# Moving context work and a layer's first groups into the preceding feed-forward in a four-layer transformer kernel

## The reference, cut to what matters

```python
# layer 0 (layer 1 has the same form), heads of 16 numbers
h1 = _modulate(_ln(x), sh_msa, sc_msa);  x = x + (_attend(qkv of h1) @ W_proj + b_proj)
h2 = _modulate(_ln(x), sh_x, sc_x);      x = x + (_attend(h2 @ W_q, ctx @ W_k, ctx @ W_v) @ W_out + b_out)
h3 = _modulate(_ln(x), sh_mlp, sc_mlp);  x = x + (gelu(h3 @ W_fc1 + b_fc1) @ W_fc2 + b_fc2)
# layer 2, heads of 64 numbers, with rotary positions
ctx_n = _ln(context, ca_lnc_w, ca_lnc_b)
k, v = jnp.split(ctx_n @ wkv, 2, axis=-1);  k = _rope(_heads(k), sk, ck)
# layer 3, heads of 64 numbers, no rotary positions
k = (ctx @ Wk).reshape(b, j, heads, -1);  v = (ctx @ Wv).reshape(b, j, heads, -1)
```

## Time and profile before

| | us |
|---|---|
| median of 3 runs | 5055.48 |
| range of the runs | 5040.6 to 5058.69 |
| the profiled execution, its time | 5061.33 |
| the profiled execution, its span from first to last instruction | 5059.5 |
| PE busy | 4276.2 (85%) |
| DVE busy | 3428.3 (68%) |
| ACT busy | 1869.3 (37%) |
| POOL busy | 1266.7 (25%) |
| mean granted TensorE clock | 0.913 |

### The profile page before, as it was taken

The page is one execution under the profiler, slowest core; times in us unless marked ns, Lnnn a source line. Parts: engine busy times, 40 slices in busy tenths (PEclk is TensorE's granted clock), DMA queues, the critical chain, the costliest instruction groups (busy, mean ns, idle before and its releaser), DMA issues.

```text
span 5059.5 us, 55363 instructions
## 1 busy us (share of the span) xinstructions
PE 4276.2 (85%) x20572; PEld 2524.0 (50%) x20572; DVE 3428.3 (68%) x4976; ACT 1869.3 (37%) x2692; POOL 1266.7 (25%) x600
## 2 busy tenths in 40 slices
PE   6899989799988778888889577777999999867769
PEld 4343357334346645545554344456555555434448
DVE  4888766788856656666668465665677777746665
ACT  2556643355644233333334222222444444412211
POOL 1000010110001245555555211111444444500010
PEclk8999989899989989999999777788999999977879
DMA  3222230222222032212222332302222232153310
GB/s 113 40 39 45 45 64 11 56 52 39 37 44 54 23 71 59 59 35 59 59 59 56 77 72 60 70 29 53 59 64 60 60 84 59 31 111 73 72 40 20
DMA packets 156283, 279.67 MB, mean 55 GB/s; under 512 B 38102, under 2 KB 70160, under 8 KB 154864
## 3 DMA queue, kind: packets, MB, share of 16 engines
q1 hardware_dynamic: 156016, 276.14, 25.8%
HBM read 99.75 MB, written 23.97 MB: 24 GB/s over the span
## 4 chain that ended last, share of the span: by engine, by line
PE 59%; DVE 17%; issue 7%; ACT 5%; SPq 5%; POOL 5%; DMA 3%; DVEq 0%; POOLq 0%; ACTq 0%
PE PS L847 23%; PE PS L1000 11%; PE PS L1043 5%; PE PS L922 4%; DVE PS L1581 3%; PE PS L1131 3%; PE PS L918 3%; DVE t L1504 3%; PE PS L1014 2%; SPq L1916 2%; PE PS L1053 2%; POOL t L1765 2%; SPq L1929 2%; DMA t<-t 2%; PE PS L957 1%
## 5 line engine op out<-in xcount | busy, mean ns | idle before, releaser
L847 PE MATMUL PS<-t 128*128 128x512 f32 (+7 forms) x7128 | 1943.0, 400 | 264.6 <-ACT t L1261 103.3
L1261 ACT ACTIVATE t<-PS 128x512 f32<-128x512 f32 (+3 forms) x1728 | 1239.9, 738 | 1511.5 <-PE PS L847 1505.4
L847 PEld LDWEIGHTS PS<-t 128*128 128x128 f32 (+4 forms) x7128 | 1158.9, 185 | 790.0 <-issue 248.9
L1000 PE MATMUL PS<-t 128*32 128x512 f32 (+3 forms) x4608 | 899.8, 620 | 0.2
L1500 DVE TENSOR_REDUCE t<-PS 128x1 fp32r<-128x1024 f32 x512 | 622.0, 1220 | 310.5 <-PE PS L918 304.7
L1504 DVE TENSOR_REDUCE t<-PS 128x1 f32<-128x512 f32 x1024 | 649.1, 684 | 79.4 <-PE PS L922 78.0
L1786 POOL TENSOR_TENSOR t<-t 128x1024 f32<-128x1024 f32 x256 | 621.6, 2428 | 147.8 <-ACT t L1261 122.9
L1581 DVE RECIPROCAL PS<-PS 128x256 f32<-128x256 f32 x256 | 449.5, 1756 | 12.5 <-PE PS L1014 12.5
L922 PE MATMUL PS<-t 96*128 96x512 bf16 x1024 | 381.7, 400 | 41.7 <-DMA t<-scr_n 19.9
L1729 POOL TENSOR_TENSOR t<-t 128x2048 f32<-128x2048 f32 x24 | 110.1, 4587 | 1190.2 <-DVE t L1400 647.9
L918 PE MATMUL PS<-t 128*128 128x512 f32 x1024 | 339.2, 415 | 65.2 <-DMA t<-t 36.5
(11 more groups left out here) (125 smaller groups left out, 3744.1 us busy)
## 6 DMA issues: line engine op xcount, KB each, us to landing
t<-t SPq DMA_DIRECT2D x512, 128.0 KB, 3.5
t<-t SPq DMA_DIRECT2D x256, 256.0 KB, 3.9
t<-scr_n SPq DMA_DIRECT2D x288, 128.0 KB, 6.1
scr_n<-t SPq DMA_DIRECT2D x72, 256.0 KB, 2.2
t<-t SPq DMA_DIRECT2D x256, 64.0 KB, 2.1
t<-in_L_Wg SPq DMA_DIRECT2D x16, 768.0 KB, 4.6
t<-in_L_W SPq DMA_DIRECT2D x36, 256.0 KB, 3.3
t<-in_L_Wo SPq DMA_DIRECT2D x64, 128.0 KB, 2.6
```

The costliest lines, as they stand in the source:

```text
L847: ins = e.matmul(out, l, r, start=i == 0, stop=i == len(terms) - 1, tile_position=tp)
L1000: ins = e.matmul(banks[S.ot][wd * j:wd * j + wd, :], u.v[j][kt], P[0:S.pr, j, :], start=kt == 0, stop=kt == S.nkt - 1, tile_position=(0, w ...
L1261: e.activation(dst, src, ACT.Exp, scale=S.L.scale).then_inc(*expd.inc((S.i, i)))
```

## The change

1. The kv stages of layers 2 and 3 disappear as stages of their own. Their steps are put into the mlp of the layer before (`kv64_steps`), keys stay on their way through `scr_k`, values now go through a DRAM buffer `scr_v` too. The reload (`kv_stack`) and the constants of `KXA` and `KXB_` stand at the start of the cross-attention. The padding rows of `VXS` and `P` are gone.
2. Layer 1's first groups (`begin16`, `p16`, `keep16`, `stack16`, the row maxima of unit 0) are put into layer 0's mlp, at positions 20 to 33.4. The values of b = 0 and the fill of the second `QK` buffer stay behind the `rest`. In layer 0 itself the same order is used ahead of its core.
3. In every mlp the layer norm of the next layer's first part is put into positions 17.65 to 23.75 (it was 17.7 to 31), and its weights to 17.1 and 18.7.
4. Memory is laid out anew, so that tiles used at different times share a place.

The core of the diff:

```diff
+    def share(c, kb, *users):
+        for user in users:
+            with ExitStack() as own:
+                user(own)
+        sbt(c, [128, 256 * kb])
...
+        share(c, 24, chances, lambda c: mlp_tiles(M, c))
+        share(c, 40, natural, *([lambda c: kv_tiles(kvs[2], c)] if L.i else []))
+        share(c, 16, second, lambda c: mlp_input(M, c))
...
+        share(c, 32, values, lambda c: mlp_weights(M, c))
...
+    def begin16_steps(S, plan, at, nat, last, lo, hi):
+        plan.put(at, 0, [("begin16", S)])
+        for ch in range(2):
+            plan.put(nat + (last - nat) * ch / 2, nat + (last - nat) * (ch + 1) / 2, nat16_steps(S, 0, ch))
+        plan.put((nat + last) / 2 + 0.01, 0, [("stack16", S, 0)])
+        plan.put(lo, hi, max_steps(S, 0))
+
+    def kv64_steps(K, plan):
+        plan.put(-3.9, 0, [("kv_load", K)])
+        plan.put(1.2, 0, [("kv64_in", K)])
+        for g in range(4):
+            plan.put(3.3 + 1.5 * g, 0, [("kv64_k", K, g)])
+        for b in range(NB):
+            for i in range(2):
+                plan.put(9.7 + 1.5 * (2 * b + i), 0, [("kv64_v", K, b, i)])
+        plan.put(8.6, 0, [("kv_keep", K)])
...
-        if L.style == 16 and S.kind == "kv":
+        if S.kind == "kv":
             continue
...
-                    plan.put(-20, -20, [("begin16", S)])
+                    if not L.i:
+                        begin16_steps(S, plan, -20, -19, -17, -9, -8)
+                    plan.put(-10, 0, [("fill16", S)])
...
-                    for ch in range(2):
-                        plan.put(-19 + ch, -19 + ch, nat16_steps(0, ch))
-                    plan.put(-18.5, -18.5, [("stack16", S, 0)])
-                    plan.put(-10, -9.5, [("val16", S, 0, t) for t in range(4)])
-                    plan.put(-9, -8, max_steps(S, 0) + [("val16", S, 0, t) for t in range(4, 8)])
+                    plan.put(-9.7, -9.2, [("val16", S, 0, t) for t in range(4)])
+                    plan.put(-8, -7, [("val16", S, 0, t) for t in range(4, 8)])
...
                 plan.put(-20, -20, [("begin64", S)])
+                if S.cross:
+                    plan.put(-19.5, 0, [("kv_stack", S.kv)])
...
-                    at = 17.7 if b else 0.9
+                    at, gap, pace = (17.65, 0.05, 0.9) if b else (0.9, 0.35, 2)
                     for t in range(8):
-                        plan.put(at + 0.35 * t, 0, [("ln_stats", p, t)])
-                    plan.put(at + 2.8, 0, [("ln_rstd", p)])
+                        plan.put(at + gap * t, 0, [("ln_stats", p, t)])
+                    plan.put(at + 8 * gap, 0, [("ln_rstd", p)])
+                    at += 8 * gap + 1
                     for q in range(4):
                         for t in range(2):
-                            plan.put(at + 2 * q + t + 4, 0, [("ln_norm", p, 2 * q + t)])
-                        plan.put(at + 2 * q + 6.3, 0, [("ln_turn", p, q)])
-                        plan.put(at + 2 * q + 7.4, 0, [("ln_split", p, q)])
-                    plan.put(at + 12, 0, [("ln_bias", p)])
+                            plan.put(at + pace * (q + t / 2), 0, [("ln_norm", p, 2 * q + t)])
+                        plan.put(at + pace * q + 0.5 * pace + 1.05, 0, [("ln_turn", p, q)])
+                        plan.put(at + pace * q + pace + 1.1, 0, [("ln_split", p, q)])
+                    plan.put(at + 4 * pace + 0.2, 0, [("ln_bias", p)])
                     for i, step in enumerate(weight_steps(p) if b else []):
-                        plan.put(at + 10 + i, 0, [step])
+                        plan.put(17.1 + 1.6 * i, 0, [step])
+                    if b and L.i == 0:
+                        begin16_steps(p.stage, plan, 20, 23.4, 28.4, 29, 33.4)
+            if L.i in (1, 2):
+                kv64_steps(kvs[L.i + 1], plan)
...
             elif what == "begin64":
...
                 if S.cross:
-                    for P in S.P:
-                        e.memset(P[64:96, :, :], 0.0).then_inc(*zeroed.inc(S.i))
+                    K = S.kv
+                    e.memset(f(K.KXA[:, :, NW:256]), 0.0)
+                    e.memset(f(K.KXB_[0:64, 1::2, :]), 0.0).then_inc(*zeroed.inc((S.i, "k")))
+                    w.wait_ge(zeroed, (S.i, "k"))
+                    e.memset(f(K.KXB_[0:1, 1::2, :]), 1.0)
+                    e.memset(f(K.KXB_[64:65, 0::2, :]), 1.0).then_inc(*zeroed.inc((K.i, "k")))
...
+            elif what == "kv_stack" and a[0].L.style == 64:
+                S, = a
+                w.wait_ge(kx_kept, S.i)
+                for blk, s in enumerate((0, 1, 0, 1)):
+                    e.dma_start(f(S.KXA[32 * blk:32 * blk + 32, :, 0:NW]), KXD[s].rearrange("(h r) n -> r h n", r=32)
+                                ).then_inc(*kx_in.inc(S.i, 16))
+                w.wait_ge(zeroed, (S.i, "k"))
...
+                for b in range(NB):
+                    e.dma_start(S.VXS[b][:, :], VD[b]).then_inc(*vx_in.inc(S.i, 16))
```

More of the change, by code:

```diff
@@ L260, in _build @@
     kx_in = signal("kx_in")
+    vx_in = signal("vx_in")
+    vx_kept = [signal(f"vx_kept{i}") for i in range(2)]
     m_in = [signal(f"m_in{i}") for i in range(8)]
@@ L402, in _build, with narrow_layer, chances, natural @@
         mods = [sbt(c, [128, L.nmod, NB]) for L in Ls]
-    kvs = {}
+    kvs = {L.i: [S for S in stages if S.L is L and S.kind == "kv"][0] for L in Ls}
+    def narrow_layer(L, c):
+        first, K, C, M = [[S for S in stages if S.L is L and S.kind == kind][0] for kind in ("self", "kv", "cross", "mlp")]
+        C.kv = K
+        K.KX = sbt(c, [128, 16, 2 * CT], BF16)
+        K.VXS = [sbt(c, [96, 16, 32]) for _ in range(NB)]
+        def chances(c):
+            first.P = [sbt(c, [128, 4, 512]) for _ in range(3)]
+        def natural(c):
+            first.NAT = sbt(c, [128, 2, 6, N], BF16)
+            first.QK = [sbt(c, [128, 2, 4, N], BF16)]
+        def second(c):
+            first.QK.append(sbt(c, [128, 2, 4, N], BF16))
+        def values(c):
+            first.VS = [sbt(c, [128, 8, 16, 32]) for _ in range(NB)]
+        share(c, 24, chances, lambda c: mlp_tiles(M, c))
+        share(c, 40, natural, *([lambda c: kv_tiles(kvs[2], c)] if L.i else []))
+        share(c, 16, second, lambda c: mlp_input(M, c))
+        attention_tiles(first, c)
+        attention_tiles(C, c)
+        kv_tiles(K, c)
+        share(c, 32, values, lambda c: mlp_weights(M, c))
@@ new lines, in wide_layer @@
+    def wide_layer(L):
+        first, K, C, M = [[S for S in stages if S.L is L and S.kind == kind][0] for kind in ("self", "kv", "cross", "mlp")]
+        C.kv = K
+        with ExitStack() as c:
+            attention_tiles(first, c)
+        with ExitStack() as c:
+            K.KXA, K.KXB_ = sbt(c, [128, 16, 256], F32R), sbt(c, [128, 16, 2 * CT], F32R)
+            K.VXS = [sbt(c, [CT, 1024]) for _ in range(NB)]
+            attention_tiles(C, c)
+        with ExitStack() as c:
+            mlp_weights(M, c)
+            mlp_tiles(M, c)
+            mlp_input(M, c)
+            if L.i == 2:
+                kv_tiles(kvs[3], c)
@@ L611, in _build @@
             S.cross = [T for T in stages if T.L is S.L and T.kind == "cross"][0]
+    for p in line:
+        p.stage = [S for S in stages if p in S.parts][0]
     order.append(("setup",))
@@ L633, in _build @@
             if L.style == 16:
-                def nat16_steps(b, ch):
-                    return [("p16", S, b, ch, half, qk) for half in range(2) for qk in range(S.nqk)] + [("keep16", S, b, ch)]
                 last = S.parts[1].next
@@ L756, in _build @@
     wkeys = list(wsets)
-    for p in line:
-        p.stage = [S for S in stages if p in S.parts][0]
     def w_prior(p, g):
@@ L1133, in tensor_program @@
             elif what == "rest":
-                then = stages[a[0] + 1] if a[0] + 1 < len(stages) else None
+                then = ([T for T in stages[a[0] + 1:] if T.kind != "kv"] + [None])[0]
                 if then and then.kind == "mlp":
@@ L1735, in gpsimd_program @@
                 e.tensor_tensor(wlo, stage, f(whi), ALU.subtract).then_inc(*w_low_p.inc((p.key, g)))
-            elif what == "begin16" and not a[0].cross:
+            elif what == "fill16":
                 S, = a
```

264 lines of the change are left out of this document (121 added, 143 removed).

## The result

The changed kernel takes 5063.8 us (median of 20 runs, 5052.99 to 5077.46), the kernel before beside it 5056.76 (20 runs, 5039.97 to 5061.78). The ratio is 1.002, 95% interval 1.0011 to 1.0029: the change costs some 10 us, less than 0.5%. I had forecast 5010, with 4980 to 5040 as range: wrong. The profiled execution took 5072.43 us (span 5070.3) against 5061.33 before (span 5059.5), 11.1 us more.

What follows compares the result with a forecast made beforehand. PE was taken to bound the mlps and chains the seams. Gains of 132.8 us at the seams less 33.4, 20.8, 21.4, 6.1 and 6 left 45.1 us: a median of 5010, range 4980 to 5040.

Steps and rivals of the forecast that it cites:

- three memsets of `P` fall away: Layer 3's cross-stage start: these savings stand against at most some 5 us of moved DVE work; net cost 2.6 us.
- Layer 0's mlp: Layer 1's first projections and maxima, a stack-DMA wait and a memset add 33.4 us there, squeezed norm apart.
- the maxima: Tail of layer 0's mlp: row maxima from position 29, bound by DVE, take 27 us instead of 11.5, 15.7 more.
- The clock in the mlps: Mlps of layers 1 and 2: after a PE wait the clock is low, costing 1.9 us in each.
- The layer norm: Three mlps: squeezing the next part's norm costs 2 us net each, 6 us in all, between −9 and 15.
- Layer 1's mlp: Moved kv work adds PE work of 11.6 and 0.8, a wait of 6.5 and clock 1.9: 20.8 us.
- Layer 2's mlp: Moved kv work adds PE work of 11.6, a 7.9 wait for the load behind the chunks, clock 1.9: 21.4 us.
- The starts of the cross stages: Layers 2 and 3: constants and reload cost 3.5 and 2.6 us, between 0 and 6 each; the reload's landing is hidden.
- Dearer waits: Rival: unknowns, mainly mlp waits in DVE's order, at their dear end: 29 us more, gain 16, about 5040; chance 0.21.
- Slower by the clock: Rival: new waits in three mlps keep TensorE at 1.2 GHz; with 80 us of such work, 5090; chance 0.07.
- the signs I set: Wrong if an mlp grows over 40 us, its middle runs at clock 0.5, or `kx_in` waits over 10 us.
- the cheap case: Rival: earlier loads, overlapping context chain and a free squeeze make waits 25 us cheaper, 4985; chance 0.17.

Runs made afterwards that it cites:

- a96: The changed kernel with the padding put back, av and sum reading 96 rows instead of 77 in the wide cross stages: 0.9965.
- e_seam: The changed kernel with layer 1's first groups and maxima kept behind the barrier, as in layer 0: 1.0012.
- best4: The changed kernel with 128 rows in av and sum, old norm spacing, earlier context load, later reload, and layer 1's first-group maxima behind the barrier: 0.9901.
- e_stack: The changed kernel with the reload of keys and values issued behind the query weights' load in both wide cross stages: 1.0004.
- best2: The changed kernel with 128 rows in av and sum (narrow cross stages' av too), old norm spacing, earlier context load, later reload: 0.9896.

## Why the prediction was wrong

**The step that failed.** It is a term put at nothing. The diff sets `S.pr` to 77, and the prediction reads it as "three memsets of `P` fall away", a small gain at the starts of the cross stages; to the cores behind these starts it gives no term. For `av` alone that is right (779 ns both), but I never asked what else hangs on the rows. a96 shows the price, 28 us with 7 either way, half of the 56 us between forecast and result (45.1 forecast, 11 lost in the profiled pair). With the rows given back (0.9965, some 5039 us) the kernel lies just inside my range, at its dear end. The other half is mostly waits and time at the low clock that the sum had too cheap, part by part below.

**Layer 0's mlp** cost 44.5 us instead of 35.4 (33.4 and a third of the norm's 6). By e_seam and best4 it divides, each to some 2 us, into 4.1 for the squeezed norm (forecast 2), 18.3 for `p16`, stack wait and memset (forecast 17.7: right), and 21.5 for the maxima. I had 15.7 for them, 27 us from their start to the end; it took 29.6. DVE bounds the tail as I said:

```profile
L1568 DVE TENSOR_REDUCE t<-PS 128x1 f32<-128x512 f32 x32 | 19.5, 682 | 2.1 <-PE PS L976 2.1
```

but behind the last maximum PE waited 2.98 us for the parts that it turns, and the last down then took 2.93 us at a granted clock of 0.53, where twelve of its matmuls took 1.67 before. By the difference, the end without maxima took some 8 us (29.6 − 21.5) and not the 11.5 that I set against it:

```profile
940.20 0.59 PE L1011 MATMUL PS<-t 128*12 128x128 bf16 x4 [2.98 <-DVE t L1610]
940.73 2.93 PE L1188 MATMUL PS<-t 128*128 128x256 f32 x12
```

The stack wait was 2.53 us (forecast 3). Behind the barrier 13.8 us were left instead of 10.5: the memset stands ahead of the values' bias on DVE, and PE waits for it:

```profile
946.32 3.47 DVE L1493 MEMSET t<- 3x4096 bf16 x1 [1.21 <-issue]
...
950.30 5.80 PE L901 MATMUL PS<-t 128*128 128x256 f32 x32 [2.56 <-DVE t L1530]
```

**The clock in the mlps.** The sum has 1.9 us for it in two mlps. The mlps of the kernel before, with 0.98, 0.98 and 0.95, became 0.93, 0.94 and 0.90:

```profile
797.70:898.80 101.10, 96.44 (x608) 86.35 (x608) 72.13 (x146) 35.97 (x55) 12.82 (x3) 0.98 0.04 12
1627.50:1728.60 101.10, 96.44 (x608) 86.49 (x608) 72.27 (x147) 35.97 (x55) 12.83 (x3) 0.98 0.04 11
3354.80:3466.60 111.80, 98.53 (x608) 87.65 (x608) 77.96 (x155) 35.95 (x55) 23.31 (x11) 0.95 0.09 29
```

In the traces 13.5 us of PE's busy time in the three mlps lay at 0.50 before, and 37.5 after. At half speed that is, by estimate, 12 us lost instead of 3.8.

**The layer norm.** The direction was right, the size not: 6 us per mlp (4.1 in layer 0's) instead of 2 net. I priced DVE's total work in the squeeze and what POOL stretches; what counts is that the first quarter's normalization stands behind eight statistics and stretched casts, and PE at its transposes. That is the 5.5 us wait. The 15 us that the prediction sets beside its 6 lie near the 16 measured (4.1, 6.0 and 5.9), but they don't come out of its working: with 8.2 for 6.8 that gives 3.5 net per mlp, some 10 in all.

**Layer 1's mlp** came out as worked, 22.6 us against 20.8 and 2, with a wait of 5.6 before the transposes (forecast 7.2). The norm's 6 stand in it, so the keys' and values' own part was some 17, 4 us cheaper. That the two misses cancel is luck.

**Layer 2's mlp**: the mechanism was right (the load behind the chunks), the size off. The load was issued where I put it, 20.8 us behind the barrier (the row load of the earlier trace rows came 21.0 behind it), but Wk landed 8.8 us behind its issue, some 3 us later than the 5.8 that I took from layer 3's kv stage, and PE waited 12.5 instead of 9.4.

**The starts of the cross stages.** Layer 2's cost nothing, 59.0 us from barrier to first exp where it took 58.4 before; I had 3.5. Layer 3's cost 11.5 (45.0 against 33.5) instead of 2.6. I wrote that the reload's landing lies beside a long chain. In layer 3 the chain is short (33.5 us against 58.4 before the change), and the load of the query weights stands behind the reload in SP's order, which waits 7.3 us for the memsets between its halves:

```profile
4445.18 1.93 SPq L2021 DMA_DIRECT2D t<-scr_k  x4
4454.43 1.78 SPq L2028 DMA_DIRECT2D t<-scr_k  x4
4456.31 0.74 SPq L2032 DMA_DIRECT2D t<-scr_v  x2
4457.10 0.84 SPq L1951 DMA_DIRECT2D t<-in_L_Wo  x2
4457.98 0.43 SPq L1894 DMA_DIRECT2D t<-in_L_caWq  x1
```

The query weights then landed 8.2 us behind their issue, where in e_stack, ahead of the reload, it took 3.3. The prediction lists what stands behind the waiting steps on SP in the mlp, but here it names only the queries' stacks. e_stack gives 5 of the 9 us back and loses 4 at layer 2's start.

**The rivals.** *Dearer waits* held: the three mlps and layer 3's start took 21 us more than I worked out, the starts of layers 1 and 2 gave 2 back, and without the rows' price the change would have gained 18 us (a96), near the 16 of that case. *Slower by the clock* had the right sign: the clock fell in the mlps, but by some 8 us more than I had priced and not by the 45 and more of that case, and it fell in the cross stages, through the rows of two matmuls, of which no rival spoke. By the signs I set, one was met: an mlp grew by over 40 us, layer 0's. One sum in the rivals is off: the cheap case counts 9 us for the squeeze, where its own bounds, 6 down to −9, are 15 apart.

## What to carry to other kernels

In these stages a padded contraction row cost a matmul no time (`sum` took 592 to 1116 ns with 77 rows and with 128) and paid for its memset several times over (5.5 us at layer 2's start, against a net gain of 28 from 77 to 96): before trimming the rows of matmuls in a stage whose granted clock is below 1, run it both ways and compare how much of the stage lies at the low level, or the mean time of the matmuls that nothing else touched. Work moved from a seam into a stage that PE fills gains only the seam's waits, and each step must be placed where the engine ahead of PE has time for it; here the squeezed norm, the order of the loads and the reload took back some 29 us, the trimmed rows 28, and four small edits brought 68. When an instruction on a queue waits in its place, list everything behind it.

## What the runs showed of the hardware

In this kernel the granted clock answers to the number of rows that two matmuls in a stage read, though the added rows of `P` hold zeros (in `av` the values beside them are zero too, in `sum` they are ones). From the first exp to the end of layer 2's cross stage the clock was 0.74 to 0.76 with 77 rows in both matmuls, 0.78 with 96 and 0.78 to 0.79 with 128; in layer 3's 0.77 to 0.79, 0.80 to 0.83 and 0.84 to 0.88, with the same matmuls and nearly the same waits. Only how long the clock stays at its low level changes: a matmul's time at either level is the same with 77, 96 and 128 rows. The Trainium skill ("TensorE: Matmul & The Clock Gate", The HAM clock gate) has the clock set by how busy TensorE has been of late; counted by matmuls and waits the engine was as busy in all these runs, so no run here shows that, and the rows made the difference. Why they do isn't shown. Whether the same holds in the narrow cross stages is open (best2), and so is where between 96 and 128 rows the effect ends: 11 us more in the changed kernel and 20 in the one before, with 9 and 7 either way.
